# Another order of loads, table switches and scalars in a one-core Perceiver layer (Trainium2)

## What is computed

```
x = x + xattn(layernorm(x), ctx)      # Q = x Wq + bq; K = ctx Wk + bk; V = ctx Wv + bv
                                      # K_hat = cos(K Wr + br); softmax(Q K_hat^T) V
x = x + attn(layernorm(x))            # per sequence: the 8 most similar earlier tokens,
                                      # softmax over q k^T there, mixed with x (log_mix),
                                      # gelu(blended * gain + bias) * (softplus(log_scale) + 0.01)
x = x + ffn(layernorm(x))             # 8 experts, each token goes to the best one only:
                                      # p_max * (gelu(h W1[e] + b1[e]) W2[e] + b2[e])
```

## Time and profile before

| what | us |
|---|---|
| median of three executions | 447.17 |
| the profiled execution | 446.33 |
| its span, first to last instruction | 444.2 |
| busy: TensorE matmul | 411.5 (93%) |
| busy: TensorE weight load | 281.9 (63%) |
| busy: ScalarE | 255.9 (58%) |
| busy: VectorE | 248.5 (56%) |
| busy: GpSimd | 237.7 (54%) |

### The profile page before, as it was taken

How to read it: one execution, slowest core, us unless ns; L and a number is a source line. 1 busy time by engine, 2 the same in 40 slices (tenths; PEclk the granted TensorE clock), 3 DMA queues, 4 the chain that set the end, 5 groups by cost and what they waited for, 6 DMA issues and landing times.

```text
span 444.2 us, 10438 instructions
## 1 busy us (share of the span) xinstructions
PE 411.5 (93%) x3121; PEld 281.9 (63%) x3121; DVE 248.5 (56%) x808; ACT 255.9 (58%) x582; POOL 237.7 (54%) x458
## 2 busy tenths in 40 slices
PE   7977999999999999999898878889999999999991
PEld 7423445454455544545344667679999999998991
DVE  2637478878988888788788655543222222222210
ACT  1474777888888988888678745253333232424240
POOL 1760567767788788888667765451222232222210
PEclk9987999999999999999999998999999999999997
DMA  9897899896986987789999624765685656465100
GB/s 174 188 251 214 216 273 273 202 214 174 278 186 150 240 202 212 185 206 260 190 296 310 220 79 132 234 173 206 239 304 187 200 180 217 165 192 198 57 0 2
DMA packets 119450, 87.46 MB, mean 197 GB/s; under 512 B 78622, under 2 KB 109088, under 8 KB 119268
## 3 DMA queue, kind: packets, MB, share of 16 engines
q1 hardware_dynamic: 111460, 75.96, 62.7%
q0 software_dynamic: 3744, 9.46, 7.0%
q10 hardware_dynamic: 4192, 1.38, 1.7%
HBM read 79.15 MB, written 8.53 MB: 197 GB/s over the span
## 4 chain that ended last, share of the span: by engine, by line
PE 71%; SPq 15%; issue 4%; DMA 4%; DVE 2%; ACT 1%; another core or an unknown queue 1%; POOL 0%; DVEq 0%; ACTq 0%; POOLq 0%
PE pK L1513 19%; PE pT L1500 17%; SPq L575 10%; PE pK L1475 8%; PE pT L1475 7%; PE b L1420 3%; SPq L570 3%; PE b L1659 3%; PE b L1554 3%; PE b L1619 2%; PE b L1598 2%; DMA f_row<-rows_by_token,token_i 2%; DMA token_i<-tokens_by_expert 2%; SPq L563 1%; PE b L1648 1%
## 5 line engine op out<-in xcount | busy, mean ns | idle before, releaser
L1272 ACT ACTIVATE XF<-pT,b_now 128x128 f32<-128x128 f32 x184 | 52.7, 370 | 97.1 <-PE pT L1500 91.8
L1513 PE MATMUL pK<-W,XF 128*128 x368 | 86.6, 387 | 5.9 <-issue 4.1
L1500 PE MATMUL pT<-XF,stage 128*128 128x128 f32 x736 | 87.0, 275 | 0.3 <-issue 0.3
L1500 PEld LDWEIGHTS pT<-XF,stage 128*128 128x128 f32 x736 | 85.9, 192 | 2.1 <-issue 1.1
L1513 PEld LDWEIGHTS pK<-W,XF 128*128 128x128 f32 x368 | 68.8, 193 | 15.5 <-issue 6.9
L409 POOL DMA_INDIRECT f_row<-rows_by_token,token_i x23 | 23.8, 1035 | 83.3 <-DMA out_dram<-XF,token_i 70.3
L1475 PE MATMUL pK<-stage,Wkr 128*128 128x512 f32 x128 | 63.0, 618 | 0.0
L1475 PE MATMUL pT<-stage,Wkr 128*128 128x512 f32 x128 | 61.8, 606 | 1.1 <-DVE stage L726 1.1
L1247 ACT ACTIVATE stage<-stage 128x512 f32<-128x512 f32 x64 | 40.7, 637 | 12.8 <-DVE stage L787 12.6
L787 DVE TENSOR_TENSOR stage<-stage 128x512 f32<-128x512 f32 x64 | 46.2, 722 | 0.7
L726 DVE STREAM_TRANSPOSE stage<-XF 128x1024 f32<-128x1024 f32 x32 | 39.5, 1234 | 12.4 <-DMA XF<-in_ctx_dram 11.3
(11 more groups left out here) (196 smaller groups left out, 666.1 us busy)
## 6 DMA issues: line engine op xcount, KB each, us to landing
stage<-in_L_ffn_W_dram SPq DMA_DIRECT2D x23, 1024.0 KB, 5.4
stage<-in_ctx_dram SPq DMA_DIRECT2D x32, 512.0 KB, 5.4
XF<-in_ctx_dram SPq DMA_DIRECT2D x248, 64.0 KB
W<-in_L_ffn_W_dram SPq DMA_DIRECT2D x8, 1024.0 KB
rows_by_token<-rows_out SPq DMA_DIRECT2D x16, 256.5 KB
ctx_last<-in_ctx_dram SPq DMA_DIRECT2D x64, 32.0 KB, 4.5
X<-in_x_dram SPq DMA_DIRECT2D x1, 1536.0 KB, 7.8
tokens_by_expert<-no_token POOLq DMA_DIRECT2D x2, 576.0 KB, 4.2
```

The source lines that it names most:

```text
L1272: ins = act.activation(f_hT[b][:, n * P:(n + 1) * P], pT[i][:, (n % 4) * P:(n % 4 + 1) * P], ACT.Gelu, bias=b1_now[:, b, n:n + 1])
L1500: mm = pe.matmul(pT[i][:, (n % 4) * P:(n % 4 + 1) * P], W1[q][:, c, n * P:(n + 1) * P], f_inT[:, q % 2, c * P:(c + 1) * P], start=c == 0, ...
L1513: mm = pe.matmul(p_out, f_hT[q % 2][:, n * P:(n + 1) * P], W2[:, bass.ds(e, 1), n, :].rearrange("p o d -> p (o d)"), start=n == 0, stop=n ...
```

## The change

- GpSimd issues the two loads of log_mix and log_scale at its start (before: ScalarE, in the prologue). own_part's zeros and diagonal are made with the masks, and only its multiplication stays in step 3.
- SP: only quarters of sequence 0 of half (1, 0); then group 0's context rows, half (1, 1), half (2, 0), group 1's context rows. bv and Wv are no longer SP's. W2 is loaded in the steps 3, 4, 5, 7, 8, 9, 11 and 13 (before: 3, 5, 7, 9, 11, 13, 14, 15). In g = 15 load_tokens(0) stands ahead of next_group.
- VectorE: half (0, 1) is transposed ahead of whole(0, 0), half (1, 0) behind fraction(0, 2). Its part of scalars moves from the end of step 1 into step 2.
- ScalarE: the Sin table, then Wq, bq and Wqk are issued ahead of Wkr's copy; then the four other quarters of half (1, 0); bv and Wv behind turn(0, 2); turn(0, 3) ahead of queries(0). The Exp table is loaded in step 1 behind turn(1, 0); scalars moves from behind first_exp(0) to the end of step 1.
- TensorE: projection (1, 0, 1) moves behind the transposes of xn, as in all other steps. value_project(0) waits for bv and Wv alone; router(0) waits for the other weights.

```diff
@@ CTX_LOADS = CC
-        W_LOADS = 4
+        W_LOADS = 3
@@ gpsimd, behind minus_half
+            for k, name in enumerate(("log_mix", "log_scale")):
+                pool.dma_start(logs[:, k:k + 1], a["L0_attn_" + name].partition_broadcast(P)).then_inc(S["logs_ld"], 16)
@@ gpsimd, masks() and own_parts()
                 made(pool.memset(unpicked[:], UNPICKED))
-                made_at["masks"] = n[0]
-
-            def own_parts():
-
                 made(pool.memset(own_part[:], 0.0))
                 for j in range(BG):
                     keep(own_part[j * T:(j + 1) * T, :], [[-1, T]], 0, 1, ALU.not_equal, 1.0)
+                made_at["masks"] = n[0]
+
+            def own_parts():
+
@@ gpsimd, s == 1
-                    pool.wait_ge(S["bv_ld"], 16)
+                    pool.wait_ge(S["bv_ld"], 2 * 16)
@@ sync, prologue
             sp.wait_ge(S["ctxT_r"], 1)
-            for j in range(2):
-                load_by_feature(1, 0, j)
+            load_by_feature(1, 0, 0)
+            load_ctx(0, 0)
+            load_last(0, 0)
             sp.wait_ge(S["ctxT_r"], 2)
             for j in range(2):
                 load_by_feature(1, 1, j)
-            load_ctx(0, 0)
-            load_last(0, 0)
-            sp.dma_start(bv[:], a["L0_xattn_bv"].partition_broadcast(P)).then_inc(S["bv_ld"], 16)
-            sp.dma_start(Wv[:], rows(a["L0_xattn_Wv"])).then_inc(S["w_ld"], 16)
-            load_ctx(1, 1)
-            load_last(1, 1)
             sp.wait_ge(S["ctxT_r"], 3)
             for j in range(2):
                 load_by_feature(2, 0, j)
+            load_ctx(1, 1)
+            load_last(1, 1)
@@ sync, the loop over g
+            W2_AT = (3, 4, 5, 7, 8, 9, 11, 13)
...
+                if g == NG - 1:
+                    load_tokens(0)
                 next_group(g, g % 2)
...
-                if g >= 3 and g % 2:
-                    load_w2(g // 2 - 1)
-                if g == NG - 1:
-                    load_tokens(0)
+                if g in W2_AT:
+                    load_w2(W2_AT.index(g))
                 if g % 2 and g >= 7:
                     keep((g - 7) // 2)
-                if g == NG - 2:
-                    load_w2(NG // 2 - 1)
@@ vector, prologue
+            ctx_turned(0, 1)
             whole(0, 0)
             fraction(0, 0)
-            ctx_turned(0, 1)
...
             last_copy()
-            ctx_turned(1, 0)
             whole(0, 2)
             fraction(0, 2)
+            ctx_turned(1, 0)
@@ vector, the loop over s
                 if s + 1 < NG:
                     next_moments(s + 1)
+                if s == 2:
+                    scalars()
...
-                if s == 1:
-                    scalars()
@@ scalar, prologue
-            act.activation(sumA[:], ident[:, 0:1], ACT.Sin)
+            load_table(ACT.Sin, 0)
+            act.dma_start(Wq[:], rows(a["L0_xattn_Wq"])).then_inc(S["wq_ld"], 16)
+            act.dma_start(bq[:], col(a["L0_xattn_bq"]), allow_slow_non_contiguous=True).then_inc(S["wq_ld"], 16)
+            act.dma_start(Wqk[0:H, :], a["L0_attn_W_q"]).then_inc(S["wqk_ld"], 16)
+            act.dma_start(Wqk[H:2 * H, :], a["L0_attn_W_k"]).then_inc(S["wqk_ld"], 16)
             act.wait_ge(S["wkr_mm"], 2)
             act.mul(Wkr[:, 1, :], pT[1][:, 0:D], INV_2PI).then_inc(S["wkr_half"], 1)
...
+            act.wait_ge(S["ctxT_r"], 1)
+            for q in range(P // T):
+                act.dma_start(*quarter_by_feature(1, 0, 1, q)).then_inc(by_feature_ld[0], 16)
@@ scalar, the first turns
             turn(0, 0)
+            turn(0, 1)
             act.dma_start(X[:, 2:4, :], x_v[:, 2:4, :]).then_inc(S["xnext_ld"], 16)
-            turn(0, 1)
             xnT_copy(0)
             sine(0, 0, 0)
...
             turn(0, 2)
+            act.dma_start(bv[:], a["L0_xattn_bv"].partition_broadcast(P)).then_inc(S["bv_ld"], 16)
+            act.dma_start(Wv[:], rows(a["L0_xattn_Wv"])).then_inc(S["bv_ld"], 16)
+            turn(0, 3)
             queries(0)
+            sine(0, 0, 2)
...
-            turn(0, 3)
-            sine(0, 0, 2)
@@ scalar, the loop over s
                 turn(s, 0)
+                if s == 1:
+                    load_table(ACT.Exp, 1)
                 xnT_copy(s)
                 first_exp(s - 1)
...
-                if s == 1:
-                    scalars()
...
                 if s == 1:
+                    scalars()
                     act.wait_ge(S["b1_tr"], 1)
@@ tensor
 value_project, g == 0:
-                    pe.wait_ge(S["w_ld"], 16 * W_LOADS)
+                    pe.wait_ge(S["bv_ld"], 2 * 16)
 router:
+                if g == 0:
+                    pe.wait_ge(S["w_ld"], 16 * W_LOADS)
 the loop over s:
                 ctx_project(s, 0, 0)
-                if s == 1:
-                    ctx_project(s, 0, 1)
                 scores(s - 1)
...
                 xn_T(s)
-                if s >= 2:
-                    ctx_project(s, 0, 1)
+                ctx_project(s, 0, 1)
```

More of the change, by code:

```diff
@@ L1319, in _ @@
             turn(0, 0)
+            turn(0, 1)
             act.dma_start(X[:, 2:4, :], x_v[:, 2:4, :]).then_inc(S["xnext_ld"], 16)
-            turn(0, 1)
             xnT_copy(0)
             sine(0, 0, 0)
-            act.dma_start(logs[:, 0:1], a["L0_attn_log_mix"].partition_broadcast(P)).then_inc(S["logs_ld"], 16)
-            act.dma_start(logs[:, 1:2], a["L0_attn_log_scale"].partition_broadcast(P)).then_inc(S["logs_ld"], 16)
             sine(0, 0, 1)
             turn(0, 2)
+            act.dma_start(bv[:], a["L0_xattn_bv"].partition_broadcast(P)).then_inc(S["bv_ld"], 16)
+            act.dma_start(Wv[:], rows(a["L0_xattn_Wv"])).then_inc(S["bv_ld"], 16)
+            turn(0, 3)
             queries(0)
+            sine(0, 0, 2)
             act.wait_ge(S["last_fr"], 4)
             act.activation(khat_last[:], last_frac, ACT.Sin, scale=TWO_PI).then_inc(S["khat_last_r"], 1)
-            turn(0, 3)
-            sine(0, 0, 2)
             sine(0, 0, 3)
```

## The result

The change makes the kernel slightly slower: 449.63 us median (20 executions) beside 445.35 (20), a ratio of 1.008, 95% interval 1.0048 to 1.0111. I had forecast 438.2 and a range of 433.8 to 443.5; the time lies above all of it, on the other side of the 445.35. The ratio leaves out the slower executions of each kernel, among them one of 1424.45 us and the profiled one, which took 450.86 us (span 448.7); what the argument takes from that trace is therefore set beside the traces of the experiments.

A forecast was written before the change was run, and what follows sets the result against it. Prologue waits on the Exp table and SP's late issues, plus the first token list's passage, were taken as the bound. Prologue 7.5 + list 1.5 - W2 0.5 = 8.5 us less, giving 438.2 us, range 433.8 to 443.5.

The forecast's parts named there:

- the prologue's 7.5 us: Up to 60 us: 8.3 us won on TensorE's path, less 0.8 for scalars at the end of step 1.
- the list's 1.5 us: First expert's token list: GpSimd no longer waits for it and the first gather may land sooner; 1.1 to 2.2 us won.
- What bounds the prologue: Up to 60 us: TensorE holes of 2.34 us (late Exp table) and 2.35 us (half (2, 0) issued late by SP).
- 8.3 summed for this path: TensorE, scores(0) to projection (2,0,0)'s end: 1.5 at the front plus 8.99 removed, less 2.18 added.
- the first hole: TensorE's 2.34 us wait ahead of the transposes of probs, to close with the Exp table loaded earlier.
- GpSimd issues the two logs while it waits for the first moments: Prologue: GpSimd's waiting covers the logs' issues; without cover, these and other added issues would cost 1 to 2 us.
- That the clock stays up is an inference: Prologue: remaining holes under 1.5 us keep TensorE's clock up; if it falls, 4.3 us are lost.
- W2 in steps 4 and 8: Moved W2 loads: 0.5 us lost, ends 0 and 5.6, from 225 GB/s needed beside 274 GB/s carried.
- SP's spare time: Steps with W2: SP has less spare time than TensorE gains; named within the term of 0.5 us lost.
- rival D: Steps 4 to 6: three W2 loads in a row make context halves late; three holes of 5.2 us, 453.8; chance 0.04.
- rival B: Prologue: transfers bind, not issues, so half the prologue's gain stays; 441.5, to 444 us; chance 0.22.
- scalars' two table loads: End of step 1: Exp and Ln each need a load; the hole ahead of probs(1) grows from 0.62 to about 1.4 us.

The follow-up runs named there:

- Experiment 7: The kernel before with Exp table early, projection (1, 0, 1) behind xn's transposes and scalars at its new place, no DMA moved: 444.67 us, 1.0011.
- experiment 5: The change with W2 in the old steps and the two logs issued by ScalarE behind sine(0, 0, 0): 442.63 us, 0.9994 against the kernel before.
- experiment 9: The change with the logs on ScalarE, and W2's steps and the list's place as before: 440.3 us beside 444.38, 0.994.
- experiment 13: The kernel before with one edit, GpSimd issues the two logs instead of ScalarE: 448.85 us beside 445.27, 1.0074.
- experiment 2: The change with W2 in the old steps: 446.72 us, 0.9989 against the kernel before.
- experiment 6: The change with W2 in the old steps and the first list behind the last context rows: 442.63 us, 0.9975 against the kernel before.
- experiment 3: The change with the first list behind the last context rows, as before: 446.69 us, 1.0106 against the kernel before.
- experiment 4: The change with Wq, bq and Wqk issued behind Wkr's copy, as before: 447.03 us, 1.005 against the kernel before.
- experiment 1: The kernel before with only W2's steps changed, to 3, 4, 5, 7, 8, 9, 11, 13: 448.7 us beside 443.68, 1.0109.
- experiment 8: The kernel before with one W2 load moved from step 15 to step 8, so three stand in a row: 447.63 us, 1.007.
- experiment 14: kernel 10 with W2 in steps 4, 6, 8, 10, 12, 14 and two loads in step 15: 440.24 us beside 445.27, 0.9872.
- experiment 11: The kernel of experiment 9 with half (1, 0) transposed ahead of whole(0, 2), as before: 439.53 us, 0.9936 against the kernel before.
- experiment 12: The kernel of experiment 9 with x in two loads, groups 4 and 5 in step 2, the rest in step 4: 440.28 us, 0.9919.
- experiment 15: The kernel before with one edit, the token list issued ahead of the last step's context loads: 450.81 us beside 445.27, 1.0103.
- kernel 10: The kernel of experiment 9 with W2 in steps 4, 6, 8, 10, 12, 13, 14, 15: 438.52 us, 0.9868 against the kernel before.

## Why the prediction was wrong

I had forecast 8.5 us less; the ratio of 1.008 is 3.6 us more. Three terms of the sum are off: the prologue's 7.5 us are not kept, the list's 1.5 us are a loss or nothing, and W2's steps cost several times the 0.5 us.

*What bounds the prologue: right.* Experiment 7 shows (2, 0) as the binding load, and experiments 5 and 9 show scores(1) 8.0 and 8.4 us ahead of before, beside 8.3 summed for this path. Inside the sum errors offset each other. SP was to issue (2, 0) from 20 to 24 us and did so from 22.56 to 28.95; VectorE came for it at 30.62 in place of 26.5, so there was no wait. Half (1, 1), which I had not looked at, was late instead and kept 1.46 us of the first hole. In the change the granted clock is 1.00 from 26 to 47 us.

*"GpSimd issues the two logs while it waits for the first moments": the cover was wrong.* I costed GpSimd's time, which is free, and not the transfers. The loads delay the first context half by 1.3 us (experiment 13), and with it SP, which waits for its transpose. VectorE's copy of Wkr stands behind that transpose, so TensorE waits 1.33 us ahead of the first projection, and the clock falls to 0.50 (13 to 15 us): 5.40 us for 8 matmuls, 3.70 before. This is the 5.0 in place of 8.3 us: the five changed prologues with the logs on GpSimd have scores(1) 4.4 to 6.0 us ahead of before, the six with the logs on ScalarE 7.9 to 8.4. (1, 1) is late in both (2.36 and 1.60 us in experiments 5 and 9). What it costs at the end is less clear. That experiment 13 loses 0.7% is measured but not explained: in its profiled execution the lateness is gone by scores(2) (59.79 beside 59.74). In the changed prologue the same edit makes no difference that the intervals show (experiments 2 and 5: 0.9989 and 0.9994; 6 and 9: 0.9975 and 0.994).

*"That the clock stays up is an inference", from holes under 1.5 us: not a rule.* The clock fell behind the hole of 1.33 us ahead of the first projection, and behind 1.37 and 1.34 in experiments 2 and 6, and stayed at 1.00 there behind 0.36 to 0.85 us (3, 4 and 13). But it stayed at 1.00 behind the change's later holes of 1.46, 1.44 and 2.01 us. The length of a hole alone doesn't decide it.

*"W2 in steps 4 and 8 ... Also SP has less spare time than TensorE gains. I take 0.5 us lost": the step that failed.* Both halves of this term are several times what I took.

The moved W2 loads cost 1.1%, 4.8 us, by themselves (experiment 1), and 0.9% in the change (1.008 beside 0.9989 in experiment 2). I averaged bytes over a step: 3.1 MB in 13.9 us is 225 GB/s, below the 274 of 60 to 80 us. In the change 144 to 158 us runs at 241 GB/s with the DMA engines at 1.04, and the half that comes next is late (2.01, 1.15, then 4.55 us). My explanation is that a step with W2 in it uses up what was ahead and the step without one restores it, so that three in a row have nothing to restore from. Experiments 1, 8 and 14 fit it; experiment 3, without the hole, shows that it doesn't strike in every execution, and how far ahead the stream is was never measured. This was rival D's mechanism, to which I gave 0.04; its place is mainly step 10, not 4 to 6, and one hole of 3.2 us with the lower clock behind it, not three of 5.2, so it ended within 2%.

SP's spare time was named and not priced. In the change SP's end of the prologue moved 0.4 us where TensorE gained 5; with the logs on ScalarE (experiment 9) it moved 3.7 us, (2, 1) from 30.70 on, where TensorE gained 8.4. In both SP falls short by 4.6 to 4.7 us, and that comes back as the hole of step 4 and smaller ones: the lead falls from 5.7 us to nothing by scores(4) in experiment 2 and from 8.4 to 4.5 in experiment 9. So of the 7.5 us that the prologue was to give, the prologue alone keeps 0.6% or 2.7 us (experiment 9, interval 1.2 to 4.1). That is near what rival B gave for its case, half of the gain. Experiments 11 and 12 rule out the transpose's place and show the eight issues of (3, 0) stretched by the 1.5 MB of x in front of them (6.20 us, and 4.15 in experiment 12 with 0.25 MB there), which is rival B's mechanism. The Trainium skill ("DMA: Bandwidth & Descriptors", Issuing engines are not separate DMA queues) says that all issuers share the same 16 engines; by that a load moved to ScalarE's or GpSimd's queue saves issue time only. The trace agrees: with loads moved off SP the DMA share from 12 to 24 us is 1.22, before 0.84, and SP's sixteen quarters there take 12.19 us where before they took 9.25.

*The list, 1.5 us won: wrong in sign.* GpSimd's wait for the list did go, as I said. What I left out stands behind SP's waiting instruction: the last context rows and b2, which then land beside the gather and W1. I had written that the rows land 4 us later and that only values(15) needs them; they need the DMA engines, at the time of the gather. By itself it costs 1.0% (experiment 15, interval 0.3 to 1.8). In the changed prologue with W2 old the difference is 0.5% (experiments 5 and 9: 0.9994 and 0.994) or 0.1% (2 and 6: 0.9989 and 0.9975), and in the change itself there is none (1.0106 without it, 1.008 with it); these intervals overlap.

*scalars' two table loads: right.* Exp and Ln each have a load of 1.28 us (38.75 and 40.59), and the hole ahead of probs(1) is 1.44 us, forecast 1.4.

So the prologue gives about 0.6% if the logs stay on ScalarE, and W2's steps, the list and the logs lose 1.1, 1.0 and 0.7% when each is put into the kernel before. These four add to a loss of 2.2%, the change loses 0.8%: I take it that one lateness hides another, which isn't shown. Taking W2's steps alone back gives 0.9989, not a gain; it takes the list and the logs too (0.994). The lowest ratio is kernel 10's, with the prologue, the old list, the logs on ScalarE and W2 from step 4 on: 438.52 us, 0.987; 14 is as good.

What stays open: how two loads of 128 x 4 bytes delay eight larger ones by 1.3 us; why experiment 13 ends 0.7% later; why the hole of step 10 varies from execution to execution; and how W2 could be spread with neither adjoining steps nor a load near the list.

## What to carry to other kernels

A load's mean rate over a step is no price for it: look at how much the stream is ahead when it comes, and at the step after it. When the compute path is shortened, move the supply by as much, or the gain returns as a hole a few steps later. A wait put earlier in an in-order DMA list holds up what is queued behind it, and DMA engines left idle there were crowded later. One trace per kernel is not enough to place a loss of 1%.

## What was not expected of the hardware

Two small loads issued by GpSimd, 2.01 to 3.4 us, move the landing of the first context half, issued by other engines, from about 8.3 to 9.7 us. Most issues on SP take 0.42 to 0.54 us, and the eight of (3, 0), right behind the 1.5 MB of x, take 0.79 on average (6.31 us, DMA share 0.93). A high DMA share alone does not do it: the four at 11.30 us take 1.80 us in a stretch with a share of 1.21. The 1 MB of the first W1 took 8.18 us to land in the changed kernel and 13.27 us in experiment 5, which differs from it in W2's steps and the logs. The granted clock fell to 0.50 behind a hole of 1.33 us and stayed at 1.00 behind one of 2.01.
